# A three-layer image kernel on one core: preparation of the next image through two PSUM banks

## The chip, the core and the metric

The kernel runs on one core of a Trainium2 chip. The core's engines work side by side and meet at semaphores: TensorE (PE; its weight loads are shown as PEld), VectorE (DVE), ScalarE (ACT), GpSimd (POOL) and SyncE (SP), which issues the DMA transfers. The metric is device time in microseconds (us) of one execution, lower is better.

## What is computed

The input x is 8 images of 16 channels, 512 x 512, float32. Four residual layers follow one another, each on a group-normalised x (8 groups of 2 channels):

```python
x = x + _L0_conv_ref(_gn(x), ...)   # rfft2, complex 3x3 convolution over the spectrum + bias, irfft2
x = x + _L1_conv_ref(_gn(x))        # two halves of the channels gate each other, per row
x = x + _L2_conv_ref(_gn(x), W)     # 3x3 convolution, 16 -> 16 channels, padding 1
x = x + _L3_conv_ref(_gn(x), weight)  # the same form again
```

The spectral layer is computed without a Fourier transform: a 3x3 convolution of the spectrum is, in space, a mix of channels with weights that depend on cos and sin of row and column, plus correction terms at the edge of the half spectrum.

## The kernel before

**Tiles.** A strip is 8 rows of 16 channels on 128 partitions, 512 columns. An image has 64 strips in SBUF (`x1`), a pair is 2 of them. PSUM (`ps`) has 8 banks of 512 columns.

**Stages of one image** (`image`, run for i = 0 to 6 in a loop with `more` true, then once more for the last image with `more` false):

1. Layer 0: `mix`, `add_u`, `turn` and `hilbert` pair by pair on TensorE. Beside this, `project_next` accumulates sums over the rows of the next image in bank 7. ScalarE's `keep` then copies them to `zz`.
2. A gap between layers 0 and 2, in which VectorE computes the statistics and gates of layer 1 with three small meetings with TensorE (`statistics`, L964, semaphores `v_sums1`, `v_sums2`). It ends with layer 2's weights (`conv_weights`, L888) and the first gate (L901).
3. Layer 2: a tail matmul (L1192) and the taps (`taps`, L1170). Each pair has a first half and a second half (the rows that come from two neighbouring strips), each of three column taps, 8 matmuls per tap and half, in all 48 matmuls of 32x32 tiles. A float32 matmul shows as two records. The second half runs LAG = 4 slots of one tap after the first, so that the first half of pair n alternates with the second half of pair n-1. DEPTH = 4 pairs of banks rotate; ScalarE evicts a pair (L553).
4. A gap, in which the statistics of layer 3 and its weights are made; TensorE computes a bias from the weights (L1217).
5. Layer 3: the same taps; ScalarE drains a pair with three activations (L564) into one of 8 slots of `cout`, and SyncE stores it.

**Preparation of the next image.** Layer 0 of image i+1 needs values that depend on its column sums `zz`: the steps are `prepare_z` (L991, L993: transposed and folded sums), `prepare_h` (L1001: Hilbert transform of the sums; L1005, L1006, L964: statistics), `prepare_u` (L1014, L1015, L1017: the edge terms u), `column_parts` (L1030), `column_turn` (L1037) and `column_sums` (L1043, L1044, L1046). VectorE's `prepare` stands between them, ScalarE keeps the results of the last three (`keep_parts`, `keep_turned`, `keep_sums`: L461, L462, L467, L473). They use banks 0, 1, 6 and 7, so layer 3 has only the banks 2 to 5 for its pairs 8 to 15 (`PREPARING = (8, 16)`, `banks3`). There the order is by passes:

```python
for n in range(*PREPARING, 2):
    for kw in range(TAPS): first3(n, kw)
    for kw in range(TAPS): first3(n + 1, kw)
    ...                                   # preparation steps between the passes
    for kw in range(TAPS): second3(n, kw)
    ...
    for kw in range(TAPS): second3(n + 1, kw)
```

Pairs 0 to 7 and 16 to 31 use the rolling form (`rolling3`). The last image has no preparation, but the same order of passes.

Each engine's instructions run in the order in which they are written; waits are on semaphores. `evicted` counts strips that ScalarE has drained, `halved` first halves that are done, `convolved` second halves, `gated` strips with their gate applied.

Of the kernel before, what the change touches and what calls it, by code (L numbers as in the profile page):

```python
# [31 lines left out]
DEPTH = 4  # L32
LAG = TAPS + 1
# [3 lines left out]
PREPARING = (8, 16)  # L37
# [150 lines left out]
Z_STEPS = 36  # L188
# [3 lines left out]
def program(nc, x, t_eye, t_hil, t_fix, t_trig, t_strip, t_rows, t_gsel, t_zsel, t_fold, t_partner, t_eye_mix,  # L192
            t_eye_conv, t_small, t_bias, w_mix, w_u, w_bias, w_conv, out):
    with ExitStack() as ctx:
# [9 lines left out]
        BU = (0, 1, 7)  # L204
        BT, BH, BE, BZ = 0, 1, 6, 7
        BY, BV, BX = 0, 4, 6
        stat = ps[:, BE, 16:32]
        BTAIL = 7
# [39 lines left out]
        u_sum = xa[2 * C:4 * C, 0, :]  # L248
# [7 lines left out]
        vsb = sb("vsb", P, 2, N)  # L256
        colv = sb("colv", P, N)[:]
# [24 lines left out]
        v_xsq = sem("x_squares")  # L282
        d_prep, v_var, a_root = sem("dve_prep_steps"), sem("var_ready"), sem("root_ready")
        a_kept, p_zt = sem("column_sums_kept"), sem("pe_zt")
        p_stat, p_zin, p_zh, p_u = sem("pe_stat"), sem("pe_zin"), sem("pe_zh"), sem("pe_u")
        v_sums0, v_zt, v_scaled, v_z, v_u = sem("sums0"), sem("zt_ready"), sem("mix_scaled"), sem("z_ready"), sem("u_ready")
# [41 lines left out]
        def banks2(n):  # L328

            return 2 * (n % DEPTH), 2 * (n % DEPTH) + 1  # L330
# [100 lines left out]
        def _(act):  # L431
# [25 lines left out]

            def keep_parts(n):

                act.wait_ge(p_cols, 3 * n + 1)  # L460
                nc.scalar.activation(vsb[0:ZR, 0, :], ps[0:ZR, BT, :], ACT.Identity).then_inc(a_cols, 1)  # L461
                nc.scalar.activation(vsb[0:ZR, 1, :], ps[0:ZR, BH, :], ACT.Identity).then_inc(a_cols, 1)  # L462
# [6 lines left out]
            def keep_sums(n):  # L469

                act.wait_ge(p_cols, 3 * n + 3)
                for q in range(2):
                    nc.scalar.activation(split_in(colv)[:, q, :], split_in(ps[:, BT, :])[:, q, :], ACT.Identity,  # L473
                                         accum_out=v1(COLQ + q)).then_inc(a_cols, 1)

            root(0, 0, 0)
# [5 lines left out]
            def image(i, more):  # L482
# [59 lines left out]
                root(i, 2, 0)  # L542
                root(i, 3, ZV)
                act.wait_ge(convolved, i * CONVOLVED + 1)
# [21 lines left out]

                with act.Fori(0, PAIRS // DEPTH) as j:
                    for e in range(DEPTH):
                        evict2(j * DEPTH + e, banks2(e))
                root(i, 4, ZV)  # L570
                act.wait_ge(v_bias3, i + 1)
                with act.Fori(0, PREPARING[0] // DEPTH) as j:
                    for e in range(DEPTH):
                        evict3(j * DEPTH + e, banks2(e), e, j)
                for n in range(PREPARING[0], PREPARING[1]):
                    if more and n == PREPARING[0] + 4:
# [4 lines left out]
                    evict3(n, banks3(n), n % DEPTH, n // DEPTH)  # L581
                    if more and n == PREPARING[0] + 1:
                        root(i + 1, 0, 0)
                        root(i + 1, 1, ZV, ZR)
                with act.Fori(PREPARING[1] // DEPTH, PAIRS // DEPTH) as j:
                    for e in range(DEPTH):
                        evict3(j * DEPTH + e, banks2(e), e, j)
# [6 lines left out]
        def _(dve):  # L594
# [81 lines left out]
            def prepare(n):  # L676

                c = Steps(dve, z_steps, n * Z_STEPS)
                dve.wait_ge(p_zt, n + 1)
                V.tensor_copy(zt.rearrange("p a b -> p (a b)"), ps[:, BZ, 0:4 * ZR]).then_inc(v_zt, 1)  # L680
                dve.wait_ge(p_zin, n + 1)
                V.tensor_reduce(v1(ZSUM, 0, ZR), ps[0:ZR, BT, :], AX_X, ALU.add).then_inc(v_sums0, 1)

                dve.wait_ge(p_stat, n + 1)
                moments(n, c, 0, stat[:, 0:2], 0)
                moments(n, c, 1, stat[0:ZR, 2:4], ZV, ZR)
# [8 lines left out]
                c.did(V.tensor_scalar(zs[0:ZR, :], ps[0:ZR, BT, :], v1(MZ, 0, ZR), v1(ZV + 1, 0, ZR), ALU.subtract, ALU.mult))  # L695
                for q in range(2):
                    c.did(V.tensor_scalar(split_in(zc[:, AXS, :])[:, q, :], ps[0:ZR, BT, HALF * q:HALF * (q + 1)], v1(MZ, 0, ZR), float(N), ALU.subtract, ALU.mult))
                dve.wait_ge(p_zh, n + 1)
                c.did(V.tensor_scalar(halves(zhs[0:ZR, :]), ps[0:ZR, BH, :].rearrange("p (q w) -> p q w", q=2), v1(ZV + 1, 0, ZR), None, ALU.mult))
                c.then(V.scalar_tensor_tensor(zg[0:ZR, :], fix[0:ZR, :], v1(MZ, 0, ZR), ps[0:ZR, BZ, 0:NG], ALU.mult, ALU.add))  # L700
                c.then(V.tensor_tensor(zg[0:ZR, :], zg[0:ZR, :], ps[0:ZR, BZ, NG:2 * NG], ALU.add))
                V.tensor_scalar(zg[0:ZR, :], zg[0:ZR, :], v1(ZV + 1, 0, ZR), None, ALU.mult).then_inc(v_z, 1)
                dve.wait_ge(p_u, n + 1)
                c.then(V.tensor_copy(ev_e[0:48, 0, :], ps[0:48, BE, 0:6]))
                part48 = lambda a, q: split_in(a)[:, q, :]
                for q in range(2):
                    w = slice(HALF * q, HALF * (q + 1))
# [21 lines left out]
            def image(i, more):  # L729
# [118 lines left out]
                if more:  # L848
                    take_next(i + 1)
# [449 lines left out]
```

## Time and profile before

| | us |
|---|---|
| median of 3 runs | 5233.11 |
| lowest and highest | 5231.74, 5235.74 |
| the profiled execution | 5223.78 |
| its span | 5222.0 |
| TensorE busy | 4715.0 (90%), mean clock 0.956 of full |
| VectorE busy | 2943.4 (56%) |
| ScalarE busy | 2477.4 (47%) |
| DMA | mean 90 GB/s |

The profile is one execution. In its timeline a row is a group of instructions of one line: start, length, engine, line, operation, output and inputs, count, and in brackets the idle time of that engine before it with what ended it. "issue" is idle time for which the profile shows no releaser. The clock is the granted TensorE clock as a share of full speed: 1.00 is 2.4 GHz, 0.50 is 1.2 GHz. Image 3 (the fourth) is shown; its layer 3 starts at 2569.15 us.

### The profile page before, as it was taken

The numbers are of one execution on the slowest core, as the hardware profiler recorded it, in microseconds if no ns is written. First come the engines' busy times: TensorE is split into PE (matmuls) and PEld (weight loads), VectorE is DVE, ScalarE is ACT, GpSimd is POOL, SyncE is SP. The second block draws the span as 40 slices with busy tenths as digits, with TensorE's granted clock in tenths as the row PEclk, the third lists the DMA queues.
The fourth block names the chain that finished last, engine by engine and source line by source line (L and its number), as shares of the span: only waits on it lengthen the run. The fifth ranks groups of instructions, "written<-read, shape, count | busy, mean of one in ns | idle before, by whom it ended". The sixth has DMA issues, their size and how long they took to land.

```text
span 5222.0 us, 222874 instructions
## 1 busy us (share of the span) xinstructions
PE 4715.0 (90%) x84800; PEld 2947.6 (56%) x84800; DVE 2943.4 (56%) x10628; ACT 2477.4 (47%) x7049; POOL 3.2 (0%) x14
## 2 busy tenths in 40 slices
PE   3799899998999899998989989899899998988889
PEld 0355555556655465555655556555555566555565
DVE  0477724767167661776527764277733777157670
ACT  4355335553455444554445544455435553344435
POOL 0000000000000000000000000000000000000000
PEclk9899899999999899998999989999899998999989
DMA  5344024430344203442134411444014440232104
GB/s 165 91 124 123 13 67 140 124 109 3 100 132 124 84 14 116 126 124 63 35 115 125 124 44 47 126 125 124 21 59 138 124 119 3 81 102 72 50 3 132
DMA packets 294838, 471.73 MB, mean 90 GB/s; under 512 B 22288, under 2 KB 97104, under 8 KB 294224
## 3 DMA queue, kind: packets, MB, share of 16 engines
q1 hardware_dynamic: 294224, 462.41, 29.6%
q8 instruction: 524, 8.59, 0.7%
q14 instruction: 90, 0.74, 0.0%
HBM read 328.10 MB, written 134.22 MB: 89 GB/s over the span
## 4 chain that ended last, share of the span: by engine, by line
PE 87%; DVE 5%; issue 3%; DMA 2%; ACT 1%; SPq 1%; ACTq 0%; DVEq 0%
PE ps L1170 33%; PE ps L1097 18%; PE ps L1082 17%; PE ps L1090 5%; PE ps L969 5%; PE ps L1106 4%; DMA shared<-t_strip 1%; PE ps L1192 1%; PE ps L1030 1%; ACT shared L564 1%; PE ps L1150 0%; SPq L377 0%; PE ps L1014 0%; PE ps L1015 0%; PE ps L1001 0%
## 5 line engine op out<-in xcount | busy, mean ns | idle before, releaser
L1170 PE MATMUL ps<-x,conv_s 32*32 32x512 f32 x49104 | 1829.9, 600 | 27.8 <-issue 20.8
L1170 PEld LDWEIGHTS ps<-x,conv_s 32*32 32x32 f32 x49104 | 1242.9, 103 | 567.2 <-issue 329.9
L1097 PE MATMUL ps<-hil,shared 128*128 128x256 f32 x4096 | 993.6, 386 | 0.0
L500 ACT ACTIVATE x<-ps,vec 128x256 f32 (+1 forms) x1024 | 490.6, 495 | 998.4 <-PE ps L1097 998.4
L1097 PEld LDWEIGHTS ps<-hil,shared 128*128 128x128 f32 x4096 | 740.4, 190 | 273.8 <-issue 194.1
L746 DVE SCALAR_TENSOR_TENSOR shared<-xin,trig 128x256 f32<-128x256 f32 x2048 | 812.7, 434 | 57.2
L564 ACT ACTIVATE shared<-ps,vec 64x512 f32<-64x512 f32 (+1 forms) x768 | 525.6, 684 | 494.2 <-PE ps L1170 483.9
L1082 PE MATMUL ps<-shared 32*32 32x512 f32 x16384 | 665.6, 614 | 0.0
L758 DVE COPY vsb<-ps 128x512 f32<-128x512 f32 x512 | 330.1, 687 | 582.5 <-PE ps L1082 582.5
L742 DVE TENSOR_SCALAR xin<-xin,vec 128x512 f32<-128x512 f32 x512 | 246.4, 481 | 614.3 <-DMA out<-shared 579.4
L553 ACT ACTIVATE x<-ps,vec 128x512 f32 x512 | 347.7, 685 | 464.4 <-PE ps L1170 464.4
L1082 PEld LDWEIGHTS ps<-shared 32*32 32x32 f32 x16384 | 312.3, 104 | 284.3 <-issue 221.9
L901 DVE TENSOR_SCALAR x<-x,cols,gate_b x1024 | 360.0, 441 | 80.4 <-issue 68.9
L1082 PE MATMUL ps<-xin,shared 32*32 32x512 f32 x8192 | 306.8, 622 | 97.9 <-DVE shared L746 58.7
L969 PE MATMUL ps<-shared 128*64 128x512 f32 x1024 | 304.8, 675 | 99.4 <-DMA shared<-t_strip 99.4
L911 DVE SCALAR_TENSOR_TENSOR work<-x 128x512 f32 (+1 forms) x512 | 331.5, 698 | 98.3 <-ACT x L553 98.3
L439 ACT ACTIVATE shared<-shared 128x512 f32<-128x512 f32 x512 | 322.4, 630 | 119.6 <-DMA shared<-x 46.0
L773 DVE SCALAR_TENSOR_TENSOR work<-x,colv 128x512 f32<-128x512 f32 x512 | 334.2, 688 | 61.5 <-ACT x L500 61.5
L1106 PEld LDWEIGHTS ps<-eye,vsb 128*128 128x128 f32 x2048 | 316.9, 202 | 58.0 <-DVE vsb L758 20.6
L511 ACT ACTIVATE shared<-x 128x512 f32 (+1 forms) x512 | 326.7, 638 | 46.0 <-ACT shared L511 44.5
L1106 PE MATMUL ps<-eye,vsb 128*128 128x128 f32 x2048 | 325.9, 282 | 18.8 <-DVE vsb L758 11.5
L493 ACT ACTIVATE shared<-ps 128x384 f32<-128x384 f32 x512 | 249.4, 487 | 106.9 <-PE ps L1106 94.0
(160 smaller groups left out, 2658.0 us busy)
## 6 DMA issues: line engine op xcount, KB each, us to landing
shared<-x SPq DMA_DIRECT2D x512, 256.0 KB
xin<-x SPq DMA_DIRECT2D x512, 256.0 KB
out<-shared SPq DMA_DIRECT2D x512, 256.0 KB
shared<-t_strip SPq DMA_DIRECT2D x576, 96.0 KB, 3.4
hil<-t_hil SPq DMA_DIRECT2D x1, 560.0 KB, 3.2
trig<-t_trig SPq DMA_DIRECT2D x1, 512.0 KB, 4.4
x<-t_bias SPq DMA_DIRECT2D x1, 512.0 KB, 5.8
x<-w_mix SPq DMA_DIRECT2D x1, 288.0 KB, 3.4
```

The lines of the kernel that those rows point to most:

```text
L500: ins = nc.scalar.activation(split_in(strip_of(s))[:, q, :], split_in(ps[:, bank, :])[:, q, :], ACT.Identity, bias=v1(MEAN), accum_out=sum ...
L553: nc.scalar.activation(strip_of(s), ps[:, banks[k], :], ACT.Identity, bias=v1(MEANP), accum_out=cols[:, 2, bass.ds(s, 1)]).then_inc(evicte ...
L564: ins = nc.scalar.activation(cout[to, o, :], ps[of, banks[k], :], ACT.Identity, bias=v1(BIAS3, to.start, to.stop))
L746: ins = V.scalar_tensor_tensor(halves_in(planes[:, a, k, :], q), halves_in(xin[:, k, :], q), 1.0, trig_of(a, q), ALU.mult, ALU.mult, accum ...
L773: V.scalar_tensor_tensor((vc, vy)[odd], strip_of(s), 1.0, colv, ALU.mult, ALU.mult, accum_out=cols[:, 2, bass.ds(s, 1)]).then_inc(dotted, 1)
L901: ins = V.tensor_scalar(of, of, cols[:, 4, bass.ds(s, 1)], gate_b[:, q, bass.ds(s, 1)], ALU.mult, ALU.add)
L911: V.scalar_tensor_tensor((vc, vs)[k % 2], strip_of(s), 1.0, strip_of(s), ALU.mult, ALU.mult, accum_out=red[:, k:k + 1]).then_inc(c_squared, 1)
L969: mm = pe.matmul(ps[HP * e:HP * (e + 1), BZ, :], strip[:, t + e, P:P + HP], xa[:, k + e, :], start=first, stop=False, skip_group_check=True)
L1082: mm = pe.matmul(ps[TM * cg:TM * cg + TM, bank, :], wst[TM * rg:TM * rg + TM, k, v, a, :], of[TM * rg:TM * rg + TM, :], start=(a == AXS), ...
L1097: mm = pe.matmul(split_in(ps[:, BY + 2 * odd + e, :])[:, int(q < 2), :], xt[:, e, q, :], hil[:, q, 0:HALF], start=False, stop=True, skip_g ...
L1106: mm = pe.transpose(ps[:, BX, q * P:(q + 1) * P], chunk(q)(vsb[:, e, :]), eye[:])
L1170: mm = pe.matmul(ps[TM * cg:TM * cg + TM, banks[k], :], conv_s[TM * rg:TM * rg + TM, kw, second, :], x1[TM * rg:TM * rg + TM, of, kw:kw + ...
```

## The change

The preparation uses banks 6 and 7 only, and is spread:

- `prepare_z` of the next image goes into the gap of layer 1, after the first statistics; `prepare_h` (without its statistics) after the second. ScalarE copies their results out of PSUM (`keep_z`, `keep_zh`) where VectorE did so or read PSUM. Layer 2's first matmul waits for these copies.
- The statistics of the next image (`prepare_stat`) go into the gap before layer 3, ahead of the bias matmuls.
- `prepare_u` becomes `prepare_u1` and `prepare_u2`, ahead of pairs 5 and 8 of layer 3; `column_parts`, `column_turn` and `column_sums` stand ahead of pairs 12, 14 and 16.
- Layer 3 runs all 32 pairs in the rolling form, on three bank pairs (`DEPTH3 = 3`) with a lag of three slots (`LAG3 = 3`). Layer 2 keeps four and four.
- `column_parts` writes its two results to different column groups; `column_sums` has one wide matmul in place of two.
- VectorE's `take_next` (L672) moves from the gap into layer 2. ScalarE's layer 3 is written out without loops.

```diff
-DEPTH = 4
-LAG = TAPS + 1
+DEPTH2, LAG2 = 4, TAPS + 1
+DEPTH3, LAG3 = 3, TAPS
...
-PREPARING = (8, 16)
+U_AT, C_AT = (5, 8), (12, 14, 16)
...
         def banks3(n):
 
-            return banks2(n if n < PREPARING[0] or n >= PREPARING[1] else 1 + n % 2)
+            return 2 * (n % DEPTH3), 2 * (n % DEPTH3) + 1
...
+            def keep_z(n):
+
+                act.wait_ge(p_zt, n + 1)
+                nc.scalar.activation(zt.rearrange("p a b -> p (a b)"), ps[:, BZ, 0:4 * ZR], ACT.Identity).then_inc(a_zt, 1)
+                act.wait_ge(p_zin, n + 1)
+                nc.scalar.activation(split_in(zc[:, AXS, :]), halves(ps[0:ZR, BT, :]), ACT.Identity, accum_out=v1(ZSUM, 0, ZR)).then_inc(a_zin, 1)
+
+            def keep_zh(n):
+
+                act.wait_ge(p_zh, n + 1)
+                nc.scalar.activation(split_in(zh_raw), halves(ps[0:ZR, BH, :]), ACT.Identity).then_inc(a_zh, 1)
+                nc.scalar.activation(zg_raw, ps[0:ZR, BZ, 0:2 * NG], ACT.Identity).then_inc(a_zh, 1)
...
+                if more:
+                    root(i + 1, 0, 0)
+                    root(i + 1, 1, ZV, ZR)
+                for n in range(PAIRS):
+                    if more and n == C_AT[0]:
                         keep_parts(i + 1)
-                    if more and n == PREPARING[0] + 6:
+                    if more and n == C_AT[1]:
                         keep_turned(i + 1)
+                    if more and n == C_AT[2]:
                         keep_sums(i + 1)
...
                 pe.matmul(stat[:, 4:6], partner[:], vec[:, EPS_Q:EPS_Q + 2], start=True, stop=True).then_inc(p_stat1, 1)
+                if more:
+                    prepare_z(i + 1)
 
                 pe.wait_ge(v_sums2, i + 1)
                 statistics(G_OUT, vec[:, ST:ST + 2], stat[:, 0:2], gsel, P).then_inc(p_stat2, 1)
+                if more:
+                    prepare_h(i + 1)
...
                 pe.wait_ge(v_conv2, i + 1)
                 due()
+                if more:
+                    pe.wait_ge(a_zh, 2 * i + 4)
+                    due()
...
                 pe.wait_ge(v_conv3, i + 1)
+                if more:
+                    prepare_stat(i + 1)
...
-                    if kw == 0:
-                        if n == DEPTH - 1:
-                            pe.wait_ge(v_bias3, i + 1)
-                            due()
-                        before = [k for k in range(n) if banks3(k) == banks3(n)]
-                        if before:
-                            pe.wait_ge(evicted, ev(i, 1 + STRIPS + 2 * before[-1] + 2))
-                            due()
+                    if kw == 0 and n >= DEPTH3:
+                        pe.wait_ge(evicted, ev(i, 1 + STRIPS + 2 * (n - DEPTH3 + 1)))
+                        due()
                     taps(n, n, banks3(n), outputs3, 0, kw)
...
+                prepare_at = dict(zip(U_AT + C_AT, (prepare_u1, prepare_u2, column_parts, column_turn, column_sums)))
+                for slot in range(PAIRS * TAPS + LAG3):
+                    n, kw = slot // TAPS, slot % TAPS
+                    if more and kw == 0 and n in prepare_at:
+                        prepare_at[n](i + 1)
+                    if n < PAIRS:
                         first3(n, kw)
...
+                    if slot >= LAG3:
+                        second3((slot - LAG3) // TAPS, (slot - LAG3) % TAPS)
```

TensorE in layer 3, before, around pairs 8 and 9 (x3 and so on count equal instructions; what an instruction waits for is in brackets):

```order
L1170 MATMUL ps<-x,conv_s 32x512 [waits evicted]
L1170 MATMUL ps<-x,conv_s 32x512 x23
L1256 REGISTER_ALU
L987 REGISTER_ALU [waits evicted]
L991 MATMUL ps<-fold,zz 128x96 [waits bias3,column_sums_kept]
L991 MATMUL ps<-fold,zz 128x96 x3
L993 MATMUL ps<-zz,fold 96x512
L1170 MATMUL ps<-x,conv_s 32x512 [waits conv_pair_halved]
L1170 MATMUL ps<-x,conv_s 32x512 x23
L1237 REGISTER_ALU
L1170 MATMUL ps<-x,conv_s 32x512 [waits conv_pair_halved]
L1170 MATMUL ps<-x,conv_s 32x512 x23
```

And after, around pair 5 (L1201 are the taps, L1036, L1029, L1030 are `prepare_u1`):

```order
L1201 MATMUL ps<-x,conv_s 32x512 [waits evicted]
L1201 MATMUL ps<-x,conv_s 32x512 x7
L1268 REGISTER_ALU
L1201 MATMUL ps<-x,conv_s 32x512 [waits conv_pair_halved]
L1201 MATMUL ps<-x,conv_s 32x512 x39
L1036 MATMUL ps<-gt,u_base 48x6 [waits z_ready]
L1036 MATMUL ps<-gt,u_base 48x6 x3
L1029 MATMUL ps<-work,u_base 48x512
L1030 MATMUL ps<-work,u_base 48x512
L1261 REGISTER_ALU
L1201 MATMUL ps<-x,conv_s 32x512 [waits evicted]
```

Passes of 24 matmuls with a wait ahead of each became runs of 48, in which `evicted` and `conv_pair_halved` are waited for 8 matmuls apart.

ScalarE's and TensorE's order in the gap of layer 1, before, has none of the next image's steps; after, TensorE's rows there are these (L980 is the statistics matmul, L1005 and L1007 `prepare_z`, L1015 `prepare_h`, L1226 the tail matmul):

```order
L1005 MATMUL ps<-fold,zz 128x96 [waits column_sums_kept]
L1005 MATMUL ps<-fold,zz 128x96 x3
L1007 MATMUL ps<-zz,fold 96x512
L980 MATMUL ps<-vec,gsel 128x2 [waits sums2]
L1015 MATMUL ps<-hil,shared 96x256 [waits zt_kept]
L1015 MATMUL ps<-hil,shared 96x256 x3
L1015 MATMUL ps<-hil,shared 96x24 x4
L1219 ISA [waits conv2_weights]
L1226 MATMUL ps<-x,conv_s 32x512 [waits zh_kept,pads_zeroed,gated]
```

TensorE in the gap before layer 3, after (L1022, L1023 and the two L980 rows behind them are `prepare_stat`, L1253 the bias):

```order
L980 MATMUL ps<-vec,gsel 128x2 [waits sums3]
L1022 MATMUL ps<-vec,zsel 128x1 [waits x_squares,zin_kept,conv3_weights]
L1023 MATMUL ps<-vec,zsel 96x1
L980 MATMUL ps<-vec,gsel 128x1
L980 MATMUL ps<-vec,gsel 96x1
L1253 MATMUL ps<-vec,conv_s 32x1 x24
L1201 MATMUL ps<-x,conv_s 32x512 [waits pads3_ready]
```

The statistics moved here from behind L1001 in layer 3, and stand ahead of the bias and of the first taps.

## Rows read from the trace of the kernel before

**Rows 1.** The page's chain of work that ended last, shares of the span by line

```profile
PE ps L1170 33%; PE ps L1097 18%; PE ps L1082 17%; PE ps L1090 5%; PE ps L969 5%; PE ps L1106 4%; DMA shared<-t_strip 1%; PE ps L1192 1%; PE ps L1030 1%; ACT shared L564 1%; PE ps L1150 0%; SPq L377 0%; PE ps L1014 0%; PE ps L1015 0%; PE ps L1001 0%
```

**Rows 2.** Timeline of PE in layer 3: start, us, engine, line, count, [idle before]

```profile
2569.15 22.45 PE L1170 MATMUL ps<-x,conv_s 32*32 32x512 f32 x578
2592.79 12.44 PE L1170 MATMUL ps<-x,conv_s 32*32 32x512 f32 x286 [1.19 <-issue]
2605.16 1.13 PE L991 MATMUL ps<-fold,zz 128*128 128x96 f32 x8
2606.13 1.02 PE L993 MATMUL ps<-zz,fold 128*96 128x512 f32 x2
2607.08 5.38 PE L1170 MATMUL ps<-x,conv_s 32*32 32x512 f32 x96
2612.39 2.58 PE L1001 MATMUL ps<-hil,shared 128*96 128x256 f32 x16
...
2615.68 7.37 PE L1170 MATMUL ps<-x,conv_s 32*32 32x512 f32 x144
2624.03 1.06 PE L1014 MATMUL ps<-work,u_base 96*48 96x512 f32 x2 [0.99 <-DVE gt L702]
...
2629.22 0.49 PE L1017 MATMUL ps<-gt,u_base 96*48 96x6 f32 x8
...
2645.57 1.21 PE L1037 MATMUL ps<-partner,vsb 96*128 96x128 f32 x8
2647.33 7.36 PE L1170 MATMUL ps<-x,conv_s 32*32 32x512 f32 x144 [0.56 <-ACT shared L564]
2654.61 1.13 PE L1043 MATMUL ps<-vsb,partner 96*128 96x512 f32 x2
...
2656.72 1.99 PE L1046 MATMUL ps<-hil,shared 128*128 128x256 f32 x8
...
2695.68 21.14 PE L1170 MATMUL ps<-x,conv_s 32*32 32x512 f32 x595 [2.01 <-issue]
```

**Rows 3.** Windows over layer 3 of images 0 to 6, their sum

```profile
sum 1025.19, PE 992.39; mean PE 141.77
```

**Rows 4.** Windows: layer 2 of image 3, layer 3 of the last

```profile
2453.64:2558.24 104.60, 104.58 (x3068) 0.99 0.02 4
5089.17:5214.26 125.09, 123.03 (x3074) 0.98 0.42 128
```

**Rows 5.** Timeline of ACT in layer 3

```profile
2577.81 2.09 ACT L564 ACTIVATE shared<-ps,vec 128x512 f32<-128x512 f32 x3 [12.23 <-PE ps L1170]
2580.93 2.09 ACT L564 ACTIVATE shared<-ps,vec 128x512 f32<-128x512 f32 x3 [1.03 <-PE ps L1170]
...
2643.99 0.59 ACT L461 ACTIVATE vsb<-ps 96x512 f32<-96x512 f32 x1 [9.35 <-PE ps L1030]
...
2645.09 4.21 ACT L564 ACTIVATE shared<-ps,vec 128x512 f32<-128x512 f32 x6
...
2716.86 2.09 ACT L564 ACTIVATE shared<-ps,vec 128x512 f32<-128x512 f32 x3 [0.48 <-PE ps L1170]
```

**Rows 6.** Timelines of PE and ACT at the end of layer 2

```profile
2455.34 102.88 PE L1170 MATMUL ps<-x,conv_s 32*32 32x512 f32 x3044
...
2558.57 0.69 ACT L553 ACTIVATE x<-ps,vec 128x512 f32 x1 [1.13 <-PE ps L1170]
```

**Rows 7.** Timeline of PE in layer 3 of the last image

```profile
5168.39 38.58 PE L1170 MATMUL ps<-x,conv_s 32*32 32x512 f32 x1140 [1.52 <-issue]
```

**Rows 8.** Timeline of PE in the gap of layer 1

```profile
2444.18 0.59 PE L964 MATMUL ps<-vec,gsel 128*128 128x2 f32 x2 [7.52 <-DVE vec L873]
2449.40 4.44 PE L1192 MATMUL ps<-x,conv_s 32*32 32x512 f32 x5 [4.63 <-DVE x L901]
```

**Rows 9.** Windows of PE: length, busy, records, granted clock, DMA share, GB/s

```profile
2456.00:2460.00 4.00, 4.00 (x83) 0.96 0.02 4
2572.00:2576.00 4.00, 4.00 (x105) 0.96 0.01 4
```

More of the change, by code:

```diff
@@ L187 @@
 MOMENTS = 5
-Z_STEPS = 36
+Z_STEPS = 32
 DVE_PREPS = 91
@@ L565, in evict3 @@
                         ins.then_inc(evicted, 1)
-                with act.Fori(0, PAIRS // DEPTH) as j:
-                    for e in range(DEPTH):
-                        evict2(j * DEPTH + e, banks2(e))
+                with act.Fori(0, PAIRS // DEPTH2) as j:
+                    for e in range(DEPTH2):
+                        evict2(j * DEPTH2 + e, banks2(e))
                 root(i, 4, ZV)
                 act.wait_ge(v_bias3, i + 1)
[L572 to L576, printed above, removed]
+                if more:
[3 more added lines that the diff above has]
+                    if more and n == C_AT[0]:
                         keep_parts(i + 1)
-                    if more and n == PREPARING[0] + 6:
+                    if more and n == C_AT[1]:
                         keep_turned(i + 1)
+                    if more and n == C_AT[2]:
                         keep_sums(i + 1)
[L581 to L587, printed above, removed]
+                    evict3(n, banks3(n), n % SLOT_PAIRS, n // SLOT_PAIRS)
             with act.Fori(0, B - 1) as i:
@@ new lines, in prepare @@
+                for a in (AXB, AXC):
+                    V.tensor_tensor(zc[:, a, :], zc[:, AXS, :], trig[0:ZR, a, :], ALU.mult).then_inc(v_zc, 1)
+                part48 = lambda a, q: split_in(a)[:, q, :]
+                dve.wait_ge(p_u1, n + 1)
+                c.then(V.tensor_copy(ev_e[0:48, 0, :], ps[0:48, BE, 0:6]))
+                for q in range(2):
+                    V.scalar_tensor_tensor(part48(vy[0:48, :], q), part48(ps[0:48, BZ, :], q), ev_e[0:48, 0, q:q + 1], part48(trig[0:48, 0, :], q),
+                                           ALU.add, ALU.mult).then_inc(v_u1, 1)
@@ L847, in image @@
                 dve.wait_ge(v_colv, i + 1)
-                if more:
-                    take_next(i + 1)
                 inverse_root(i, c, 2, 0)
                 c.settle()
-                S, Q, D, GA, A_, B_, T1, T2 = (cols[:, k, 0:STRIPS] for k in range(8))
+                S, Q, D, GA, A_, B_ = (cols[:, k, 0:STRIPS] for k in range(6))
+                T1, T2 = work[:, 2, 0:STRIPS], cols[:, 7, 0:STRIPS]
                 c.then(V.tensor_tensor(v1(SV), v1(SVQ), v1(SVQ + 1), ALU.add))
@@ L1028, in column_parts @@
                         for k in range(3):
-                            rows = slice(32 * k, 32 * k + 32)
-                            mm = pe.matmul(ps[rows, (BH, BT)[v], :], mix_s[rows, k, v, a, :], zc[rows, a, :], start=(a == 0), stop=(a == 2), skip_group_check=True)
+                            rows = slice(TM * k, TM * k + TM)
+                            to = rows if v else slice(TM * k + TM, TM * k + 2 * TM)
+                            mm = pe.matmul(ps[to, (BE, BZ)[v], :], mix_s[rows, k, v, a, :], zc[rows, a, :], start=(a == 0), stop=(a == 2), skip_group_check=True)
                 mm.then_inc(p_cols, 1)
             def column_turn(n):
-                pe.wait_ge(a_cols, 5 * n + 1)
+                pe.wait_ge(a_cols, 6 * n + 1)
                 for q in range(4):
@@ L1051, in _ @@
             prepare_h(0)
-            prepare_u(0)
+            prepare_stat(0)
+            prepare_u1(0)
+            prepare_u2(0)
             column_parts(0)
@@ L1193, in image @@
                 mm.then_inc(convolved, 1)
-                for slot in range(PAIRS * TAPS + LAG):
+                for slot in range(PAIRS * TAPS + LAG2):
                     n, kw = slot // TAPS, slot % TAPS
@@ L1213, in image @@
                 pe.wait_ge(v_conv3, i + 1)
+                if more:
+                    prepare_stat(i + 1)
                 for t in range(TILES):
```

149 lines of the change are left out of this document (60 added, 89 removed).

## The prediction

> **What bounds the kernel now.** I read the page's chain of work first: lines of TensorE fill it, the taps of the two convolutions (L1170) ahead of all with 33% of the span [rows 1]. So the question is what TensorE does in each stage. Next its timeline over one image, around the third layer's convolution ("conv3") [rows 2]: from the first tap at 2569.15 to the last one's end at 2716.82 it takes 147.7 us. Over the seven images that prepare a next one conv3 takes 1025.19 in all, mean 146.46 [rows 3]. The convolution of the second layer ("conv2") issues the same taps, 48 matmuls or 96 records a pair of strips, and takes 104.60; conv3 of the last image, which prepares nothing, takes 125.09 [rows 4].
>
> The 42 us between 104.6 and 146.5 have two parts. A rolling pair mixes its first halves with the second halves of the pair before; by the code these stand on the sixteen different 32x32 tiles of the array. ScalarE, which follows TensorE, drains such a pair each 3.1 us (2577.81, 2580.93) [rows 5], and 104.60/32 gives 3.27 with ramps and cold start. While conv3 has only two bank pairs, a pass runs alone, on eight tiles, and 96 records take 5.38 us, record ends included [rows 2]; start to start about 5.2. Eight such pairs cost 8 x (5.2-3.1) = 17 us, and one more ramp down and up about 3: this is the 20.5 us by which 125.09 stands over 104.60. The other 21 us are the preparation itself.
>
> **Conv3 after the change.** Everything rolls. I start from 104.6. The lag is three slots and not four: two half-filled slots fewer, -0.7, so 103.9. Four terms come on top.
>
> (a) The ring of three bank pairs. Pair n may start when ScalarE has drained pair n-3, whose last tap was issued three slots earlier, one pair's time or 3.10 us. The loop: last tap 0.60; ScalarE's start 0.04 after its end (2716.82, 2716.86) to 0.35 (2558.22, 2558.57) [rows 2, 5, 6]; three activations 2.09; restart of TensorE 0.14 (the third of six activations ends at 2645.09+2.10 = 2647.19, the tap starts at 2647.33) [rows 2, 5]. Sum 2.87 to 3.18 against 3.10. I take 0.05 us a pair, nearer the cheap end because ScalarE's start is close to the tap's end in one row and the average of both ends fits into 3.10: 29 pairs, 1.5 us. Bounds: 0, and 0.35 a pair (10 us) if each restart also loses its head start on loading weights. The wait for the first half of a pair ("halved") has 32 records, 1.05 us, issued behind what it waits for, against 0.60+0.14: no stall, with 0.3 us spare.
>
> (b) Stops marked "issue", with nothing in the profile behind them: 1.19 and 2.01 us in this conv3 [rows 2], 1.52 in the last image [rows 7], all in rolling stretches. That is 3.2 us on 24 rolled pairs, 4.4 on 32 with the slower records about them; last image 2.0. Bounds 2 and 7.
>
> (c) Preparation that stays in conv3, at its own time plus 0.5 each time the sixteen tiles must run empty for a matmul of another shape. From L1014 at 2624.03 to L1017 at 2629.22 six matmuls take 0.86 each; L1017's four take 0.4. U1, two of them and the small four: 2.6. U2, four: 3.9. Column parts: 18 small matmuls, so far on three tiles, now on six at once, a third of them in sequence, 3 x 0.86 and a ramp: 2.8 (bounds 2.6 and 5.2). Turn: 1.21+0.5 = 1.7. Sums: one wide matmul of two goes; 1.12+1.99+0.4 = 3.5 [rows 2]. Sum 14.5.
>
> (d) ScalarE's copies between drains. It rests 1.03 us a pair [rows 5], so a block of copies costs what exceeds that. The turn waits for the first copy: 0.8 to the drain's start, drain 2.09, copy 0.5 (L461, 0.59 with its overlap), restart 0.14, against 3.1: 0.4. The sums wait so for the turned copy: 0.5. The last two copies: 0.1. In all 1.0; bounds 0 and 4.
>
> VectorE's chain from the sums of squares to U1 is 2615.68 to 2624.03, 8.4 us, with TensorE idle 0.99 at its end [rows 2]. It now starts near 2571, and U1 stands five pairs in, near 2587. U2 and the parts follow three and four pairs later, 9 and 12 us, for 2 and 5 us of VectorE. No wait there; where this cover fails R3 prices it.
>
> Sum: 103.9+1.5+4.4+14.5+1.0 = 125.3 against 146.5: **-21.2**.
>
> **The gap between layers 1 and 2.** TensorE waits there 7.52 us for VectorE, to 2444.18, and 4.63 more to 2449.40 for the first gate [rows 8], at clock 0.50. prepare_z needs only what ScalarE wrote at the end of layer 0. Its 1.13+1.02 us [rows 2] double at that clock: 2436.7 to 2441, inside the first wait, and ScalarE's two copies (0.6 each, as L461) end before 2444. Nothing, as VectorE's statistics are not delayed. prepare_h follows at 2444.77: L1001's 2.58 us [rows 2] become 5.1, to 2449.9, then the copies 0.6+0.2 and 0.14. The first tail matmul, which uses the same bank, starts near 2450.9 and not 2449.40: +1.5. The clock rose at about 2456.3 [rows 9]; the added matmuls may bring that forward, which is worth half of the time gained on it. I take **+1.3**, bounds -1.5 and +2.5. VectorE's reduce of the squares ran beside ScalarE's root and moves into layer 2, off the path: nothing.
>
> **The gap between layers 2 and 3.** prepare_stat took at most 0.86 us of the 3.29 between L1001's start and the next tap at 2615.68 [rows 2]. It now stands behind the wait for conv3's weights, on the path, at clock 0.50: 1.7 us. The clock rises at about 2572.3 [rows 9] whichever work fills the time before, so conv3 has that much less of its work in the slow stretch and gets half back: **+0.8** (bounds 0.5 and 1.7). ScalarE's two roots now stand ahead of its first drain; VectorE gives them by 2572, and the drain comes at 2577.8 [rows 5]. Nothing.
>
> **The boundary** to the next image keeps its order on every queue, SyncE's too: nothing.
>
> Per image -21.2+1.3+0.8 = -19.1, seven times -133.5. Last image, no preparation: 103.9+1.2 (its colder start)+1.5+2.0 = 108.6 against 125.1, -16.5. Image 0's preparation is the same chain with one more handover, under +1. In all **-149**. The profiled execution is 5223.78 us with a span of 5222.0, so 5075 for a like one. The runs' median, 5233.11, is 9 above it: **5084**.
>
> **A rule against this.** L991 starts at 2605.16, where the taps before it end (2592.79+12.44 = 2605.23); L993 ends at 2607.15 and a tap starts at 2607.08 [rows 2]. The switch costs lost overlap and no more. The Trainium skill, TensorEngine Tiling, section Key Properties, says that changing the tiling mode drains the TensorE. The trace agrees with a drain. Were each of the eight switches an image charged a whole tap of 0.6, and not 0.5 a visit, 20 us of the gain would go.
>
> **Rivals.**
> R1, the ring is the bound. At the loop's upper end, 3.18, and with the head start on weights lost at each restart, a pair takes 3.4 and not 3.15: 0.25 x 29 x 8 = 58 us back, **5142**. For it: the loop has almost no slack. Against: after the idle 1.19 us rolling goes on at its pace.
> R2, slower than before. Two waits in a row ("evicted", eight matmuls, "halved") leave the queue empty at every pair, and each pays a completion and a restart. It decides at 149/(31 x 8) = 0.60 us a pair above my 3.15; 0.60+0.14 and a ring stall of 0.06 would be 0.8, 198 us, **5282**. For it: the shorter lag. Against: 1.05 us of matmuls are queued at that wait unless the ring has just run dry.
> R3, preparation late or dear. VectorE's chain or ScalarE's copies stop TensorE for 3.5 us twice an image, or switches and parts cost half as much again: +7 x 7 = 49, **5133**.
> R4, the gap pays. The clock rises earlier before layer 2, parts overlap the taps, the ring costs nothing: -2.8-1.3-1.5 an image, **5045**.
>
> **Chances.** Forecast 0.64, R1 0.17, R3 0.08, R4 0.07, R2 0.04. The range goes from two thirds of the way to R4 up to R1: **5058 to 5142**. A measurement here can tell about 0.2%, 10 us: faster 0.95, within it 0.01, slower 0.04; only R2 is not faster.
>
> **What would show it.** Right: conv3 near 125 us in images 0 to 6 and 109 in the last; ScalarE's drains each 3.1 to 3.2 us throughout; the first tail matmul 1.5 us later behind VectorE's last step; the first conv3 tap 1.7 us later; no idle time before U1 and the column parts. Wrong: drains 3.4 us apart; ScalarE as releaser of TensorE at most pairs; conv3 over 135.

## The result, and the profile after

The changed kernel takes 5066.86 us, median of 4 runs (5058.23 to 5076.03), against 5233.67 us of the kernel before in 4 runs (5231.74 to 5235.74): a ratio of 0.9688, 95% interval 0.9676 to 0.9701. The forecast was 5084, range 5058 to 5142. The profiled execution of after is 5067.6 us long with a span of 5065.8, that of before 5223.78 and 5222.0: 156.2 us less, where the sum had said 149.

The page of after: the busy time of each engine (share, instructions), the chain of work that ended last, and the group of the taps (busy us, mean ns | idle us before them), with the same group of before beneath it.

```profile
PE 4614.4 (91%) x84784; PEld 2945.6 (58%) x84784; DVE 2926.5 (58%) x10596; ACT 2499.3 (49%) x7097; POOL 3.2 (0%) x14
...
PE ps L1201 33%; PE ps L1124 18%; PE ps L1109 17%; PE ps L1117 5%; PE ps L985 5%; PE ps L1133 4%; DMA shared<-t_strip 1%; PE ps L1226 1%; PE ps L1015 1%; PE ps L1177 1%; PE ps L1029 0%; SPq L381 0%; PE ps L980 0%; PE ps L1030 0%; DMA out<-shared 0%
...
L1201 PE MATMUL ps<-x,conv_s 32*32 32x512 f32 x49104 | 1720.8, 602 | 32.8 <-issue 32.7
...
L1170 PE MATMUL ps<-x,conv_s 32*32 32x512 f32 x49104 | 1829.9, 600 | 27.8 <-issue 20.8
```

The chain is the one of [rows 1] with the line numbers moved: taps L1201 (before L1170), tail matmuls L1226 (before L1192). TensorE is still the bound. The same 49,104 tap records cover 1720.8 us in place of 1829.9, at the same 0.60 us each: more of them run side by side. The line of ScalarE's drains, 1% of the chain in [rows 1], is no longer among those that the page lists.

TensorE's windows over layer 3 of after: image 0, image 1 and image 6 (one near the mean, one of the longest, and the last that prepares, which is also the shortest), their sum over images 0 to 6, and the last image. Columns: length, busy, records, granted clock, DMA share, GB/s.

```profile
682.31:806.97 124.66, 121.14 (x3148) 0.98 0.42 128
1293.56:1422.27 128.71, 122.50 (x3148) 0.98 0.43 126
...
4342.17:4463.48 121.31, 119.38 (x3148) 0.98 0.43 132
sum 875.70, PE 847.56; mean PE 121.08
...
4946.48:5058.05 111.57, 106.79 (x3074) 0.98 0.46 144
```

The sum 875.70 is 125.10 an image, against 1025.19 or 146.46 in [rows 3]: 21.36 less. The last image has 111.57 where [rows 4] have 125.09. Of the 156.2 us, layer 3 gave 163.0 (149.5 in images 0 to 6, 13.5 in the last). The gap of layer 1 took 7.9 more and the gap of layer 2 11.2 more, layer 2 itself (from its tail's first matmul to the end of its last tap) took 7.0 less, and layer 0 with the time up to the next statistics 5.4 less.

TensorE's timeline in image 3 of after, with the rows that answer to [rows 8] and [rows 2]: the gap of layer 1, the gap of layer 2, and conv3.

```profile
2377.41 2.00 PE L1005 MATMUL ps<-fold,zz 128*128 128x96 f32 x8
2379.20 1.77 PE L1007 MATMUL ps<-zz,fold 128*96 128x512 f32 x2
2385.07 0.59 PE L980 MATMUL ps<-vec,gsel 128*128 128x2 f32 x2 [4.10 <-DVE vec L887]
2385.52 4.87 PE L1015 MATMUL ps<-hil,shared 128*96 128x256 f32 x16
2391.58 4.44 PE L1226 MATMUL ps<-x,conv_s 32*32 32x512 f32 x5 [1.19 <-ACT vsb L473]
...
2509.03 0.59 PE L1022 MATMUL ps<-vec,zsel 96*128 96x1 f32 x2 [4.22 <-DVE conv_s L902]
...
2510.61 2.16 PE L1253 MATMUL ps<-vec,conv_s 128*32 128x1 f32 x48
2512.71 17.32 PE L1201 MATMUL ps<-x,conv_s 32*32 32x512 f32 x419
2530.76 1.08 PE L1201 MATMUL ps<-x,conv_s 32*32 32x512 f32 x13 [0.73 <-issue]
2531.77 0.52 PE L1036 MATMUL ps<-gt,u_base 96*48 96x6 f32 x8
...
2547.44 12.98 PE L1201 MATMUL ps<-x,conv_s 32*32 32x512 f32 x381
...
2569.26 1.21 PE L1063 MATMUL ps<-partner,vsb 96*128 96x128 f32 x8
...
2577.70 1.04 PE L1201 MATMUL ps<-x,conv_s 32*32 32x512 f32 x2 [0.64 <-issue]
2578.67 1.12 PE L1069 MATMUL ps<-vsb,partner 128*128 128x512 f32 x2
2579.63 1.89 PE L1071 MATMUL ps<-hil,shared 128*128 128x256 f32 x8
...
2615.79 20.75 PE L1201 MATMUL ps<-x,conv_s 32*32 32x512 f32 x591 [1.35 <-issue]
2643.97 2.02 PE L1109 MATMUL ps<-xin,shared 32*32 32x512 f32 x32 [7.43 <-DVE shared L761]
```

prepare_z (L1005, L1007) runs inside a wait that was there anyway: the time from the first statistics to the second is 8.96 us in before and in after. prepare_h (L1015) stands after VectorE's last step and ahead of the tail. In conv3 neither U1 (L1036) nor the column parts, turn (L1063) and sums (L1069, L1071) wait for VectorE: the 0.99 us before L1014 in [rows 2] has no successor. What stops the taps now is "issue", for which the profile names no releaser.

ScalarE's timeline in the rolling part of the same conv3 (the drains, L588, with its wait for TensorE):

```profile
2591.40 2.09 ACT L588 ACTIVATE shared<-ps,vec 128x512 f32<-128x512 f32 x3 [1.06 <-PE ps L1201]
2594.57 2.09 ACT L588 ACTIVATE shared<-ps,vec 128x512 f32<-128x512 f32 x3 [1.08 <-PE ps L1201]
2597.58 2.09 ACT L588 ACTIVATE shared<-ps,vec 128x512 f32<-128x512 f32 x3 [0.92 <-PE ps L1201]
```

3.17 and 3.01 us from drain to drain, 3.09 on average over pairs 16 to 23 of this image, as with the full ring in [rows 5] (3.12). The ring of three bank pairs costs nothing that this row can show.

### The profile page after: what moved, and what is told of

It is laid out like the page before. It is cut to its first block, busy times and chain, and to the rows that moved or that the text cites. A ratio compares the mean times of both kernels' runs of the same rounds, so it can differ in the third digit from the quotient of the medians.

```text
span 5065.8 us, 222775 instructions
## 1 busy us (share of the span) xinstructions
PE 4614.4 (91%) x84784; PEld 2945.6 (58%) x84784; DVE 2926.5 (58%) x10596; ACT 2499.3 (49%) x7097; POOL 3.2 (0%) x14
## 3 DMA queue, kind: packets, MB, share of 16 engines
q8 instruction: 524, 8.59, 0.7%
## 4 chain that ended last, share of the span: by engine, by line
PE 88%; DVE 4%; issue 3%; DMA 2%; SPq 1%; ACT 1%; ACTq 0%; DVEq 0%
PE ps L1201 33%; PE ps L1124 18%; PE ps L1109 17%; PE ps L1117 5%; PE ps L985 5%; PE ps L1133 4%; DMA shared<-t_strip 1%; PE ps L1226 1%; PE ps L1015 1%; PE ps L1177 1%; PE ps L1029 0%; SPq L381 0%; PE ps L980 0%; PE ps L1030 0%; DMA out<-shared 0%
## 5 line engine op out<-in xcount | busy, mean ns | idle before, releaser
L1201 PE MATMUL ps<-x,conv_s 32*32 32x512 f32 x49104 | 1720.8, 602 | 32.8 <-issue 32.7
L1201 PEld LDWEIGHTS ps<-x,conv_s 32*32 32x32 f32 x49104 | 1231.3, 103 | 490.0 <-issue 248.3
L588 ACT ACTIVATE shared<-ps,vec 64x512 f32<-64x512 f32 (+1 forms) x768 | 525.7, 685 | 442.7 <-PE ps L1201 432.2
```

The costliest lines, as they stand in the source:

```text
L588: ins = nc.scalar.activation(cout[to, o, :], ps[of, banks[k], :], ACT.Identity, bias=v1(BIAS3, to.start, to.stop))
L1201: mm = pe.matmul(ps[TM * cg:TM * cg + TM, banks[k], :], conv_s[TM * rg:TM * rg + TM, kw, second, :], x1[TM * rg:TM * rg + TM, of, kw:kw + ...
```

## The experiments

The kernel before was run beside each group of kernels on the same chip: it took 5228.2 us beside e0, e1, e2 and e5, 5225.61 (one run) beside e3 and e4, and 5221.01 beside e6, e7 and e8. Differences between times are taken within a group, unless said otherwise.

### How much slack has the ring? (e0, e1, e5)

e0 is the changed kernel once more, for comparison.

> The changed kernel once more, as the base for the runs beside it on the same chip. About 5067 us, ratio 0.968 to 0.970 to the kernel before.

Measured: 5073.55 us, median of 5; ratio 0.9704, interval 0.9691 to 0.9718. Layer 3 averages 124.38 us in images 0 to 6 and 116.69 in the last one. So the last image's conv3 moves by 5 us between two executions of one kernel (it holds six stops marked "issue" of 8.0 us in all here, four of 4.8 in after), and a single one is no measure of a term of 1 us.

e1 lengthens the lag of the second halves by one slot, so that a slot's first half waits for a drain that starts only after the slot before it:

```
-DEPTH3, LAG3 = 3, TAPS
+DEPTH3, LAG3 = 3, TAPS + 1
```

> The changed kernel with a lag of four slots in layer 3, still three bank pairs. Pair n-3's last tap is then issued two slots (2.07 us) ahead of pair n, and not three (3.10). Theory A (the ring's loop is 2.9 us: last tap 0.60, ScalarE's start 0.15 to 0.3, three activations 2.09, restart 0.14; it just fits into 3.10): each pair takes 2.9+1.03 = 3.9 to 4.0 us, layer 3 some 24 to 27 us longer in each image, the kernel about 5270, and TensorE's idle time is released by ScalarE. Theory B (the loop is much shorter, or overlaps the queue, and has 1 us of slack): no change, 5067.

Measured: 5133.62 us in one run, 60 above e0 and far under the 5270 expected, and layer 3 averages 133.87 us in images 0 to 6, 9.5 above e0 and not 24 to 27. ScalarE's timeline of e1, in the last image:

```profile
5085.30 2.09 ACT L588 ACTIVATE shared<-ps,vec 128x512 f32<-128x512 f32 x3 [1.46 <-PE ps L1201]
5088.85 2.09 ACT L588 ACTIVATE shared<-ps,vec 128x512 f32<-128x512 f32 x3 [1.46 <-PE ps L1201]
5092.41 2.09 ACT L588 ACTIVATE shared<-ps,vec 128x512 f32<-128x512 f32 x3 [1.46 <-PE ps L1201]
```

A steady beat of 3.55 us: a loop is the bound here, of the kind I had described. But it is 0.38 us shorter than the sum of its steps gave. The trace shows which step: after TensorE has waited for the drain, a slot's 32 records start within 0.57 us, not within the 1.03 of a stream that is never empty. With 0.74 for the last tap and ScalarE's start, 2.09 for the drain and 0.15 for the restart, that is 3.55. In the changed kernel this slot stands outside the loop, by the code: the last tap that a pair waits for is issued ahead of the wait before it. What is left, 0.74+2.09+0.15 = 2.98 us, fits into the 3.09 of a pair with 0.1 us in hand, inside the 2.87 to 3.18 of my sum.

e5 shortens the lag by one, so that the wait for the first half has nothing of TensorE's issued behind it:

```
-DEPTH3, LAG3 = 3, TAPS
+DEPTH3, LAG3 = 3, TAPS - 1
```

> The changed kernel with a lag of two slots in layer 3: second halves then wait for a first half that was issued just ahead of them, while the ring has a slot more room. It measures the wait for halved by itself. Theory A (completion 0.60 and restart 0.14 are paid in full when nothing is queued, and are hidden at three slots where 1.05 us is queued): 0.6 to 0.75 us a pair, 3.7 to 3.85 us a pair, 150 to 190 us in all, 5220 to 5255. Theory B (the wait is free, since the matmuls of a tile are in order anyhow): 5067 or a little less.

Measured: 5176.52 us in one run, 103 above e0, where 150 to 190 were expected. TensorE's timeline of e5, in the last image:

```profile
5087.29 3.43 PE L1201 MATMUL ps<-x,conv_s 32*32 32x512 f32 x96 [0.15 <-PE ps L1201]
5090.88 3.43 PE L1201 MATMUL ps<-x,conv_s 32*32 32x512 f32 x96 [0.15 <-PE ps L1201]
```

Here TensorE waits for itself at every pair, the mechanism of R2, and a pair takes 3.59 us: 0.50 more than 3.09. In the rolling part of image 3 it is 3.6 to 3.8 us; over the whole kernel the 103 us come to 103/(31 x 8) = 0.42 us a pair. R2 was to decide at 0.60 us. Even with the wait fully bare, the kernel stays 52 us faster than before (5228.2). This run has a slot more room in the ring, so it prices the wait for the first half alone, without the ring stall of 0.06 that R2 added to it.

### Does the last image's gain come from rolling? (e3)

e3 is the kernel before, with the last image rolling through all 32 pairs over four bank pairs, as it has nothing to prepare:

```
+                if not more:
+                    rolling3(0, PAIRS)
+                    return
                 rolling3(0, PREPARING[0])
```

> The kernel before with layer 3 of the last image in rolling order over four pairs, lag four; images 0 to 6 as they were. Theory A (pass-by-pass order costs 17 us and its ramps 3 in that image, and the ring of three pairs costs nothing beside one of four): layer 3 of the last image falls from 125.1 to 105 to 112, the same as the 111.6 of the changed kernel up to the number of issue stops; pairs at 3.09 to 3.10 us in both. Theory B (the ring of three costs 0.05 a pair or more): pairs at 3.05 or less here, and layer 3 1.5 us or more shorter than the changed kernel's at equal stops.

Measured: 5214.12 us in one run against 5225.61. The window over layer 3 of its last image:

```profile
5092.76:5205.10 112.34, 107.46 (x3074) 0.98 0.45 143
```

112.34 with a ring of four (0.3 above the expected range) and 111.57 in after with a ring of three, with 4.9 and 4.8 us of stops. As the last image moves by 5 us between executions (e0), the pairs without a stop are the better measure: 3.05 us with four, 3.08 with three, and in the runs without any stop, below, 3.05 with four (e8) and 3.06 with three (e4). The ring's depth costs 0.03 a pair at most, and the last image's gain from 125.09 [rows 4] is what rolling brings, 12.8 us here. I had put the eight pairs at 17 and the ramps at 3; without the stops, below, the two kernels' last images lie 15.4 apart.

### What are the stops marked "issue"? (e4, e8)

Of the 32.8 us for which after's taps let TensorE stand idle, 32.7 have no releaser in the profile. e4 is the changed kernel, and e8 the kernel before, with each of layer 3's output stores cut to an eighth: 16 of the 128 rows of a slot go out, and seven eighths of the output are left unwritten. Both have the same edit:

```
-  sp.dma_start(out[i].rearrange(...)[j * SLOTS3 + k], cout[:, k, :])
+  sp.dma_start(out[i].rearrange(...)[j * SLOTS3 + k][0:1], cout[0:C, k, :])
```

> The changed kernel storing 16 of the 128 rows of each output strip (the rest of the output is left out). Theory A (the stops marked issue in layer 3 are instruction supply that queues behind the output stores, since layer 2 issues the same matmuls without any store and has none): the stops of 1.2 to 2.8 us, two to four an image, go, layer 3 falls from 125.1 on average to 117 to 119, the kernel to about 5015. Theory B (they come from the place in the program, loop ends or the amount of code): they stay, 5067.

> The kernel before, storing 16 of the 128 rows of each output strip (the rest of the output is left out), to set beside e4_small_stores. Theory A (the stops in layer 3 come from instruction supply beside the stores in both kernels, and the kernel before meets fewer of them only because a pass on eight tiles asks for instructions at half the rate): no stops of this kind, layer 3 at 142 to 143 us in images 0 to 6 and 120 to 122 in the last, so the change is worth 24 us an image without stores where it is worth 21.4 with them. Theory B (the stops belong to the changed kernel's new order): layer 3 stays at 146.

Measured: e4 4994.02 us, e8 5160.23, one run each. The taps' group, the sum of layer 3 over images 0 to 6, the window of the last image, and a row of image 3's timeline, of e4:

```profile
L1201 PE MATMUL ps<-x,conv_s 32*32 32x512 f32 x49104 | 1700.2, 602 | 0.0
...
sum 827.83, PE 827.75; mean PE 118.25
...
4884.11:4987.92 103.81, 103.80 (x3074) 0.97 0.11 23
...
2549.04 52.45 PE L1201 MATMUL ps<-x,conv_s 32*32 32x512 f32 x1584
```

The same three views of e8:

```profile
L1170 PE MATMUL ps<-x,conv_s 32*32 32x512 f32 x49104 | 1813.4, 600 | 7.2 <-ACT shared L564 7.2
...
sum 993.28, PE 979.06; mean PE 139.87
...
5034.81:5154.05 119.24, 119.23 (x3074) 0.98 0.09 20
```

With the small stores TensorE does not stop once for "issue" in 49,104 tap records, where after has 32.7 us of such idle time, and 1584 records run through in one piece. The stops hang on the output stores. What they cost is more than their idle time, as records around them are slower too:

| layer 3, us an image | images 0 to 6 | last image |
|---|---|---|
| before | 146.46 | 125.09 |
| before, small stores (e8) | 141.90 | 119.24 |
| after | 125.10 | 111.57 |
| after, small stores (e4) | 118.26 | 103.81 |

The stores cost 4.6 and 5.9 us an image in before, 6.8 and 7.8 in after. (e8 without them lies 0.1 and 0.8 us under its expected ranges.) So the change is worth 23.6 us an image where nothing stops TensorE, and 21.36 where something does. Both kernels gained more than layer 3 shows: e4 came 21 us under its expected 5015. In its profile layer 0 of all images, with the time up to the next statistics, is 19 us shorter than in after and the end of the program 3.4, so the full stores cost time in these stages too.

What stops TensorE can be read from the traces. The stops come at fixed places of the program. The next rows are the three stops of image 3 in e0; after, above, has its three before the same groups of 13, 2 and 591 records.

```profile
2527.93 1.08 PE L1201 MATMUL ps<-x,conv_s 32*32 32x512 f32 x13 [0.50 <-issue]
...
2575.22 1.04 PE L1201 MATMUL ps<-x,conv_s 32*32 32x512 f32 x2 [0.49 <-issue]
...
2613.33 20.54 PE L1201 MATMUL ps<-x,conv_s 32*32 32x512 f32 x591 [1.35 <-issue]
```

Counted in TensorE's instructions (matmuls, weight loads and those of its sequencer), neighbouring stops of one conv3 of after stand 255 to 257, 1791 to 1793, 2048 or 2305 apart: multiples of 256, give or take one. And the page of after has a DMA queue of instructions (packets, MB, share):

```profile
q8 instruction: 524, 8.59, 0.7%
```

8.59 MB in 524 packets are 16 KiB each, which would be 64 bytes for each of 256 instructions. In conv3 of after such packets come every 4.8 us on average. Each of the 26 stops there ends 1.35 to 1.60 us after the landing of one; so do all 148 others in before, e0, e2, e3, e6 and e7 (1.34 to 1.66). So TensorE stops for want of instructions that land late beside the stores. The packets themselves are no slower there: in layer 3 they take 1.04 us each in after and 1.13 in e4. So they start late, and what holds them back is what stays open.

### Does the clock rise at its own time? (e2, e7)

e2 moves prepare_stat in the gap between layers 2 and 3 ahead of the wait for conv3's weights, into time in which TensorE stands idle. Its output moves to bank 7, so it also waits for the copies out of that bank:

```
+                if more:
+                    prepare_stat(i + 1)
                 pe.wait_ge(v_conv3, i + 1)
-                if more:
-                    prepare_stat(i + 1)
...
-        stat_z = ps[:, BE, 24:28]
+        stat_z = ps[:, BZ, 64:68]
...
+                pe.wait_ge(a_zh, 2 * n + 2)
```

> The changed kernel with prepare_stat ahead of the wait for layer 3's weights, in the 4.2 us in which TensorE waits there (its output goes to bank 7, since VectorE reads bank 6 at that time). Theory A (in the changed kernel it stands on the path at clock 0.50, and by pushing the first tap 1.7 us later it also makes the low clock last one step longer): the bias matmul comes 1.6 to 1.7 us earlier after layer 2's end in images 0 to 6, the first tap within 11.5 us of it as before the change, the low clock of that gap lasts 10.2 us and not 13.7 in most images, and the kernel gains 7 x (1.7+0.5) = 15 us, about 5052. Theory B (the small matmuls only take the place of work that would have run at the low clock anyway, as the prediction had it): a gain of 7 x 0.8 = 6 us.

> e2_stat_early once more, as the base for e6_tail_early on the same chip: ratio 0.965 to 0.967 to the kernel before, about 5050.

Measured: e2 5052.54 us, median of 5, ratio 0.966 (0.9647 to 0.9674), 21 below e0; e7, the same kernel on another chip, 5048.35, ratio 0.9668 (0.9655 to 0.9681). Both intervals lie below that of e0. TensorE's timeline of e2 in the same gap:

```profile
2499.09 0.58 PE L980 MATMUL ps<-vec,gsel 128*128 128x2 f32 x2 [4.03 <-DVE vec L946]
2499.54 0.56 PE L1023 MATMUL ps<-vec,zsel 96*128 96x1 f32 x2
...
2503.90 2.16 PE L1254 MATMUL ps<-vec,conv_s 128*32 128x1 f32 x48 [2.73 <-DVE conv_s L902]
2505.99 9.56 PE L1202 MATMUL ps<-x,conv_s 32*32 32x512 f32 x205
```

The statistics' matmuls now end before VectorE's weights come, and the first tap stands 10.9 us behind the end of layer 2's last tap, as in before, not 12.5. Clock windows of after in its gap:

```profile
2512.00:2516.00 4.00, 4.00 (x51) 0.50 0.03 6
2516.00:2520.00 4.00, 4.00 (x100) 0.85 0.00 0
```

In after the clock is at 0.50 (1.2 GHz) until about 2517.2, 4.8 us after the first tap on average; in before it rose 3.3 us after it ([rows 9]: 0.96 already in the window from 2572). The stretch at 1.2 GHz in this gap is 13.65 us long in all seven images of after and in six of e0's, 10.24 in the seventh of e0 and in all seven of before, of e2, of e7 and of e6. The other runs agree: 20 of 21 images of e1, e4 and e5, which have prepare_stat behind the wait, show 13.65, and all 14 of e3 and e8 show 10.24. So prepare_stat cost its own 1.6 us, and then a later clock, half of 1.3 to 1.5 us. That is about 2.3 us an image. With it removed the kernel takes 21 us less, of which 7 x 2.3 = 16 are accounted for; I put the other 5 down to chance, as the medians of two kernels can differ by that much. Over images 0 to 6, the gap in the profiles of e2 and e7 is 11 us shorter than in e0's, and layer 3 is 1.7 and 5.7 us shorter.

The last image prepares nothing, its gap is 10.6 to 10.9 us in every kernel, and yet its stretch is 13.65 us long in eight of the eleven traces (before and e0 among them) and 10.24 in three. So something else can make the clock late as well, and no run here shows what.

The Trainium skill, TensorE: Matmul & The Clock Gate, Part 1, states that the throttled rate is the default and that activity releases it. The trace agrees that TensorE leaves the idle gap at the low rate. That the release came later in images 0 to 6 when prepare_stat stood between that gap and the taps is what the runs here add.

### The gap of layer 1 (e6)

e6 is e2 with prepare_h's output in bank 5 and the tail's in bank 6, so that the tail waits for prepare_z's copies alone:

```
-        BT, BH, BE, BZ = 0, 1, 6, 7
+        BT, BH, BE, BZ = 0, 5, 6, 7
-        BTAIL = 7
+        BTAIL = 6
...
-                    pe.wait_ge(a_zh, 2 * i + 4)
+                    pe.wait_ge(a_zin, i + 2)
...
+                            if more and n == 2:
+                                pe.wait_ge(a_zh, 2 * i + 4)
+                                due()
```

> e2_stat_early with prepare_h writing bank 5 in place of bank 1 and the tail matmul of layer 2 writing bank 6 in place of bank 7, so that only pair 2 of layer 2, and not the tail matmul, waits for ScalarE's copies of prepare_h. Theory A (in the changed kernel the tail stands 1.2 us behind those copies, on the path): the first tail matmul starts 1.1 to 1.2 us earlier after the first statistics, without idle time released by ScalarE, 7 x 1.2 = 8 us less, about 5042. Theory B (an earlier start falls into the low clock, and the clock then rises as before): half of that or nothing, 5046 to 5050.

Measured: 5037.66 us, median of 5 (5024.93 to 5052.95), ratio 0.9645 (0.9629 to 0.9662), against 5048.35 of e7. TensorE's timeline of e6 in the gap of layer 1:

```profile
2373.89 4.87 PE L1015 MATMUL ps<-hil,shared 128*96 128x256 f32 x16
2378.69 4.47 PE L1227 MATMUL ps<-x,conv_s 32*32 32x512 f32 x5
```

The tail follows prepare_h with no wait: the 1.19 us for ScalarE's copy (L473) are gone, and over images 0 to 6 the tail starts 0.7 to 1.3 us earlier behind the first statistics than in after, 1.1 on average, about as expected. But layer 2 took 108.71 us an image in its profile against 107.55 in e7's, which gives it all back, as theory B had it. These two profiles are a poor match: e6's is the slowest of its five runs, e7's the fastest of its own. The medians differ by 10.7 us with overlapping intervals. That e6 has the lowest median of all kernels measured is so; that its edit is the reason stays open.

## Why the prediction was right, and where it was not

**Conv3 of images 0 to 6: forecast 125.3, measured 125.10.** The sum is right to 0.2 us by luck: two errors of the opposite sign cancel, which the runs without stops take apart. Without stops the sum said 120.9 (103.9+1.5+14.5+1.0), and e4 measured 118.26.
- Term (a), the ring, 1.5 us: nothing. 3.09 us a pair in the rolling part, 3.05 with four bank pairs (e3), 3.06 in e4, and no wait for ScalarE. The loop's steps were right. I had left ScalarE's start between 0.04 and 0.35 us and charged 0.05 a pair for the upper part of this; it is 0.15 (e1), the loop takes 2.98, and so it fits.
- Terms (c) and (d), preparation 14.5 and ScalarE's copies 1.0: 14.2 together, by the length of each pair that carries a part less 3.1. U1 2.6 (forecast 2.6), U2 4.0 (3.9), parts 2.8 to 3.1 (2.8), turn with its wait 1.64 (1.7+0.4), sums with theirs 3.15 (3.5+0.5). As a check, conv3 of e4 takes 118.26 in images 0 to 6 and 103.81 in the last, which prepares nothing: 14.45 apart. The loss of overlap at each change of shape is 0.5 a visit, as I took it; the whole tap for each of eight switches that the rule against the change could have meant was not charged. The copies' waits cost almost nothing.
- Term (b), stops, 4.4: 6.8 (125.1-118.3). I had counted little more than the bracketed idle times: 3.2 us on 24 pairs are 4.3 on 32, and 0.1 for slower records. In after 4.0 an image are idle time, and slower records make up the rest. e8 shows that before already paid 4.6 an image where its "issue" rows have 20.8 us over eight images, 2.6 each. The error was to take the idle time for the whole cost.

**Last image: forecast 108.6, measured 111.57.** Without stops 103.81 against 106.6: no ring term, and hardly a colder start (its first pair takes 5.1 us in e4, 4.8 on average in the others). With stops 7.8 and not 2.0: [rows 7] had one stop of 1.52 us, and a mean from one image's brackets was too thin a base.

**Gap of layer 1: forecast +1.3.** The order came as written: prepare_z free inside the wait, prepare_h on the path. The tail starts 1.3 us later behind the last statistics in most images (6.5 us, before 5.2) and 1.1 on average, against 1.5. The half that the clock may give back varied. In images 0, 2 and 6 a stretch at 2.4 GHz began with the end of prepare_h and covered the tail's first 1.5 to 2 us, and layer 2 took 107.1; in images 1, 3 and 5 it fell on idle time, and layer 2 took 108.7 (before: 108.8 on average). In image 3 TensorE did nothing while it had the full clock:

```profile
2381.00:2384.00 3.00, 0.00 (x0) 1.00 0.00 0
2384.00:2388.00 4.00, 2.93 (x8) 0.51 0.00 0
```

Over seven images this term came to +0.35 us each in after's profile (8.0 more up to the tail, 5.5 less in layer 2) and to +1.1 in e0's, where layer 2 is 0.1 shorter than before's.

**Gap of layer 2: forecast +0.8, measured 1.6 at the first tap and about 2.3 with the clock.** The step that failed reads "The clock rises at about 2572.3 whichever work fills the time before". It rose later when prepare_stat filled it, so nothing was given back, and another 0.7 was lost. This is the only reason of the prediction that was wrong in kind; it is worth about 10 us, and e2 undid it. What sets the time of the rise stays open, as the last image shows.

**The boundary: forecast nothing.** Layer 0 with the time up to the next statistics took 5.4 us less in all in after's profile and 4.2 less in e0's. In e3, where nothing of it was changed, it took 2.7 less, so half of this may be chance.

**From the profile to the median.** 9 us were added because before's profiled execution lay that far under its median. After's lay at its median, and its four runs spread over 18 us. Of the 17 us between 5084 and 5066.86, 7 are the sum's and the rest this offset. That the sum came within 7 us of the whole is luck in part, too: the last image gave 3 less than forecast, the gap of layer 2 about 6 less, and layer 2, layer 0 and the gap of layer 1 made up for it.

**Rivals.** R1's 3.4 us a pair did not come (3.09). R2 is refuted by the result, and e5 shows that its wait costs less than it needed; R3 is refuted by the lack of any wait before U1 and the parts. R4 came true in two of its three parts: the ring is free, and the clock gave something in layer 1 in some images.

## What to carry to other kernels

An insertion into a rolling sequence costs its own time and one loss of overlap, about 0.5 us here; a phase that gives up rolling pays for every pair of it (5.2 us against 3.1), so place the work singly between pairs. Put small matmuls ahead of a wait rather than behind it, where their inputs allow it: behind it they cost their time at the low clock, and here the clock rose later as well. Idle time in brackets is a lower bound of what a stop costs: to price it, take its cause away. And where a stop has no releaser, compare its end with the landings of the instruction queue.

## What the runs showed of the hardware that I had not expected

- TensorE runs out of instructions beside output stores: 32.7 us of idle time in 49,104 tap records with 128-row stores at 128 GB/s in layer 3, 0.0 with 16-row stores at 21 GB/s, and 6.8 us an image with the slower records around the stops. All 26 stops of after end 1.35 to 1.60 us behind the landing of a 16 KiB packet of the instruction queue, and stand on multiples of 256 instructions.
- After a wait, 32 records start within 0.57 us, against 1.03 in a full stream (e1).
- Waiting for its own last result costs TensorE 0.50 us a pair in the last image and 0.42 over the whole kernel (e5), not the 0.74 of a completion and a restart in a row.
- The stretch at 1.2 GHz after layer 2 was 10.24 or 13.65 us, never between. In images 0 to 6 it was 13.65 in 33 of 35 with prepare_stat (1.6 us) behind the wait, and 10.24 in 42 of 42 without it there; in the last image it was 13.65 in 8 of 11 with no prepare_stat in any.
